# Fourteen scatter sends of the second part moved among the last attention slots, and the last batch's steps moved up to six slots later

## The chip, the core and the metric

The kernel runs on one core of one Trainium2 chip. TensorE multiplies matrices into PSUM, VectorE and ScalarE read PSUM and work elementwise, GpSimd works on SBUF and issues indirect DMAs, SyncE issues other DMAs. Each engine works through its own list of instructions in order; semaphores tie them together. The metric is the device time of one execution in microseconds (us).

## The reference

One transformer layer on x of 8 batches x 512 tokens x 128 channels: x = x + attention(layernorm(x)), then x = x + mixture(layernorm(x)).

```python
y = einsum('bnd,hde->bhne', x, Wkqv) + bkqv        # 16 heads; k and q of 128, v of 8
A = softmax(where(tril, q @ k.T / sqrt(128), -inf))
x = x + (A @ v).reshape(...) @ Wp + bp
# feed-forward on layernorm(x)
shared = (silu(x @ shared_gate.T) * (x @ shared_up.T)) @ shared_down.T
probs = sigmoid(x @ router_w.T + routing_bias)     # 8 experts
scores, indices = top_k(probs, 2); scores /= sum(scores)
combined = sum over the two picked experts of score * down(silu(gate(x)) * up(x))
x = x + shared + combined
```

## The kernel before

`prepare` loads and turns weights and is not touched. `body` holds everything else as one loop over slots `t`, from 0 to `SLOTS` = 215, written out once for each engine: an engine's list is what its code issues in slot 0, then in slot 1, and so on. Which step stands in which slot is fixed by tables of numbers; there is no scheduler.

**Attention**, slots 0 to 137. A unit is one head of one batch, 128 units. TensorE projects unit t in slot t (`project`), scores it for the row maxima one slot later, and scores it again ten slots later (`score`, three pieces, lines L1058 to L1060); VectorE takes the maxima (L1455), ScalarE the exponentials (L1327), GpSimd masks them in the same slot as the exponentials (L931 and L933). Every fourth slot, at `PV_AT + 4 g`, the value matmuls of four units follow (L1075, `weigh_values`); the last two groups stand in slots 135 and 139. They wait for the masks (`p_masked`). ScalarE copies their result (L1317) and stores it to `o_dram`. Slots 128 to 137 have no projection left.

**After attention, by batch.** When a batch's 16 heads are through, its steps run in slots `step_at(name, b)`: the gather of products and sums from DRAM, the inverse sums (`rinv`, L1514), their spread over partitions, the product (`mult`), the projection with Wp (`proj`, L1102) and its sum into x (L1394), the layer norm (`stats`, `aggr`, `newton0` to `newton2`, `norm` into `hn`), the split into two halves of 16 bits (`split`, into `rows`), and the router logits (`logits`). For the last batch, 7, the table is `LAST_STEPS`; its gather is issued by GpSimd (L946, L947), its spread is a matmul (L1108, step `spread`), its normalised rows are turned by TensorE (L1113, step `late`), copied in `late_copy`, and its exponentials (`exp`) are taken together with batch 6's on ScalarE, between two loads of the activation table.

**Routing, by part.** The tokens are cut into three parts of 12, 12 and 8 tiles of 128 (`SPLITS`). For each, VectorE picks two experts per token in seven steps (`sort`, L1552 to L1569), TensorE counts and ranks (`count`, L1132; `rank`, L1142 and on), VectorE works out each token's place (`place`, L1581 to L1600), and GpSimd scatters the rows to `xs_dram`, one indirect DMA (L969, a send) for each tile and pick: 24, 24 and 16 sends. `plan_sends` puts them in slots from `part_step_at("send", g)` on, two a slot before slot 138 and three in two slots after it. The scatter waits for `place_ready`; after slot 138 every second send also waits for TensorE's unit of the slot before (`gate_up`).

**Feed-forward**, slots 138 (`FFN_AT`) to 214. There are 69 units: 53 of routed rows, two tiles of 128 rows of one expert each, then 16 of the shared expert. A quad is four tiles; SyncE transposes its rows from `xs_dram` into a ring of four (L892). In slot 138 + u TensorE does the gate and up matmuls of unit u (`up`, L1164 to L1166, 12 matmuls) and the down matmuls of unit u - 4 (`down`, L1202 to L1204, 12 matmuls); ScalarE does Silu (L1358) and a rounding (L1363), VectorE a product (L1639) and a difference (L1642). ScalarE copies each finished quad out of its output bank (L1353) and stores it. Two output banks take turns by job, but the second also serves the small matmuls of the table `T_USES` and joins only after the last of these (`T_LAST`). `plan_fetches` then gives the 64 indirect DMAs that bring routed results back (L978, fetches) the places from `FETCH_AT` on that have no send, three in two slots; every second one of slots up to 207 waits for the unit of the slot before. VectorE adds each to x with its weight (L1610, two for a tile), those of the last eight tiles after the loop, and SyncE stores a batch when it is complete (L896).

## Time and profile before

| | |
|---|---|
| median of 3 runs | 705.58 us (703.97 to 706.2) |
| the profiled execution | 704.36 us, of which the span is 702.6 us |
| mean granted TensorE clock | 0.975 |
| busy share of the span | TensorE 91%, VectorE 77%, ScalarE 65%, GpSimd 44% |
| chain that ended last | TensorE 73%, VectorE 11%, issue 5%, ScalarE 4%, GpSimd 1% |

Times in the rows below are us from the start of the span. A row of a timeline has the start, the duration, the engine, the line, the operation, out<-in and a count, and in brackets how long the engine was idle before it and what ended that ("issue": nothing that the profile shows; "remote": no source known). PE is TensorE, DVE VectorE, ACT ScalarE, POOL GpSimd. Starts of matmuls are recorded, their ends are modelled. Slot 138's gate and up matmuls begin at 504.57.

### The profile page before, as it was taken

What the parts mean: (1) busy time and instruction counts of PE and PEld (TensorE: products, weight loads), DVE (VectorE), ACT (ScalarE), POOL (GpSimd) and SP (SyncE); (2) the same over time, 40 slices, a digit from 0 to 9 for tenths busy, and PEclk for the clock granted to TensorE, in tenths of its full rate; (3) what the DMA queues carried; (4) which work ended last, traced back from release to release, by engine and by line L of the source; (5) the groups of instructions that cost most, each with busy time, mean ns of one, the idle gap of its engine ahead of it and who ended that gap; (6) DMA issues with size and microseconds to landing.
All of it is one profiled execution on the core that took longest, in us unless ns stands there. A gap on an engine that the chain in (4) does not pass through costs nothing.

```text
span 702.6 us, 16427 instructions
## 1 busy us (share of the span) xinstructions
PE 638.1 (91%) x5432; PEld 402.7 (57%) x5432; DVE 538.8 (77%) x1903; ACT 456.4 (65%) x816; POOL 307.8 (44%) x511
## 2 busy tenths in 40 slices
PE   7489999999999999998999999999986788898983
PEld 7255555555555555554455555555565577786653
DVE  5799877798788878799878877878257745576886
ACT  3367776767767768776677866776745545565651
POOL 4393631323133223223478422422664276546673
PEclk9699999999999999999999999999999999999996
DMA  9200543621121112211241110211553376794424
GB/s 253 68 1 3 158 133 110 176 86 47 51 77 46 35 33 84 55 56 39 58 133 65 54 52 17 57 38 41 118 119 107 83 133 129 146 176 91 113 58 131
DMA packets 102768, 60.24 MB, mean 86 GB/s; under 512 B 44568, under 2 KB 94640, under 8 KB 102688
## 3 DMA queue, kind: packets, MB, share of 16 engines
q1 hardware_dynamic: 66144, 28.22, 16.7%
q10 hardware_dynamic: 32336, 22.29, 11.1%
q0 software_dynamic: 4208, 8.69, 4.8%
q8 instruction: 47, 0.77, 0.5%
q14 instruction: 33, 0.27, 0.1%
HBM read 19.62 MB, written 30.77 MB: 72 GB/s over the span
## 4 chain that ended last, share of the span: by engine, by line
PE 73%; DVE 11%; issue 5%; ACT 4%; another core or an unknown queue 1%; POOL 1%; ACTq 0%; DVEq 0%; POOLq 0%
PE bank L1058 9%; PE bank L1037 9%; PE bank L1075 9%; PE bank L1060 8%; PE bank L1059 8%; PE bank L998 4%; PE bank L1166 4%; PE bank L1000 4%; PE bank L999 4%; PE bank L1164 3%; PE bank L1165 3%; DVE junk L1455 2%; PE bank L1202 2%; PE bank L1204 2%; PE bank L1203 2%
## 5 line engine op out<-in xcount | busy, mean ns | idle before, releaser
L1327 ACT ACTIVATE p_sb<-bank,inv_scale 128x512 f32<-128x512 f32 (+1 forms) x384 | 222.1, 614 | 43.2 <-PE bank L1060 35.0
L1455 DVE CUSTOM_DVE_ANT_0 junk<-bank,causal 128x512 bf16<-128x512 f32 (+3 forms) x512 | 222.0, 483 | 29.0 <-PE bank L1037 27.5
L931 POOL TENSOR_SCALAR_AFFINE_SELECT p_sb<-p_sb 128x384 f32<-128x384 f32 x128 | 66.8, 522 | 280.3 <-ACT p_sb L1327 279.4
L1059 PE MATMUL bank<-ql,ah 128*128 128x512 f16 (+3 forms) x512 | 153.1, 299 | 0.0
L1060 PE MATMUL bank<-qh,al 128*128 128x512 f16 (+3 forms) x512 | 152.7, 299 | 0.0
L1058 PE MATMUL bank<-qh,ah 128*128 128x512 f16 (+3 forms) x512 | 146.9, 300 | 0.3 <-ACT p_sb L1327 0.3
L1037 PE MATMUL bank<-ah,qh 128*128 128x512 f16 (+3 forms) x512 | 130.1, 300 | 1.2 <-DVE low L1455 1.2
L1427 DVE TENSOR_TENSOR ql<-bank,qh 128x512 f16<-128x512 f32 x128 | 88.3, 690 | 42.8 <-ACT qh L1292 40.5
L1292 ACT ACTIVATE qh<-bank 128x512 f16<-128x512 f32 x128 | 76.4, 597 | 34.4 <-PE bank L1000 33.0
L1639 DVE SCALAR_TENSOR_TENSOR al<-bank,gu_scale,ah 128x512 f32<-128x512 f32 x69 | 51.6, 748 | 59.5 <-ACT ah L1358 43.1
L978 POOL DMA_INDIRECT p_sb<-ys_dram,place x64 | 67.9, 1061 | 39.6 <-PE bank L1166 17.4
L1358 ACT ACTIVATE ah<-bank,inv_gate 128x512 f32<-128x512 f32 x69 | 47.3, 686 | 58.3 <-PE bank L1166 32.9
L969 POOL DMA_INDIRECT xs_dram<-rows,place x64 | 65.6, 1024 | 40.5 <-issue 14.1
L1075 PE MATMUL bank<-p_sb,v_sb 128*9 128x512 f32 (+3 forms) x1024 | 74.9, 433 | 0.3 <-POOL p_sb L933 0.3
L1058 PEld LDWEIGHTS bank<-qh,ah 128*128 128x128 f16 x512 | 50.1, 98 | 38.5 <-issue 6.9
L1037 PEld LDWEIGHTS bank<-ah,qh 128*128 128x128 f16 x512 | 50.2, 98 | 35.4 <-issue 2.8
L1164 PE MATMUL bank<-mh,wh 128*128 128x256 f16 x212 | 59.4, 280 | 6.3 <-issue 4.7
L1060 PEld LDWEIGHTS bank<-qh,al 128*128 128x128 f16 x512 | 50.1, 98 | 24.9
L1166 PE MATMUL bank<-mh,wl 128*128 128x256 f16 x212 | 59.4, 280 | 3.4 <-issue 3.3
L1059 PEld LDWEIGHTS bank<-ql,ah 128*128 128x128 f16 x512 | 50.1, 98 | 20.5
L1202 PE MATMUL bank<-wh,qh 128*128 (+1 forms) x276 | 53.7, 227 | 8.5 <-issue 3.5
L1165 PE MATMUL bank<-ml,wh 128*128 128x256 f16 x212 | 59.3, 280 | 1.6 <-issue 1.4
(246 smaller groups left out, 1127.0 us busy)
## 6 DMA issues: line engine op xcount, KB each, us to landing
o_dram<-oT ACTq DMA_DIRECT2D x32, 256.0 KB, 2.3
ys_dram<-ql ACTq DMA_DIRECT2D x25, 256.0 KB
xs_dram<-causal ACTq DMA_DIRECT2D x6, 832.0 KB, 4.5
wst<-in_Wkqv SPq DMA_DIRECT2D x8, 264.0 KB, 5.0
x_sb<-in_x SPq DMA_DIRECT2D x8, 256.0 KB, 6.1
out<-x_sb SPq DMA_DIRECT2D x8, 256.0 KB
o_all<-o_dram SPq DMA_DIRECT2D x7, 256.0 KB
r_all<-r_dram SPq DMA_DIRECT2D x7, 256.0 KB
```

Source lines behind the costliest of these rows:

```text
L1037: last = nc.tensor.matmul(m.psum[M_BANK[k]][:, at:at + w], qh[:, u % RING, i * P:(i + 1) * P], m.ah[:, seg(b, N, w)], start=True, stop=True)
L1058: nc.tensor.matmul(bank, m.ah[:, keys], qh[:, s, c * P:N], start=True, stop=False)
L1059: nc.tensor.matmul(bank, m.ah[:, keys], ql[:, s, c * P:N], start=False, stop=False)
L1060: last = nc.tensor.matmul(bank, m.al[:, keys], qh[:, s, c * P:N], start=False, stop=True)
L1075: last = nc.tensor.matmul(m.psum[O_BANK][32 * j:32 * j + V1, c * P:N], m.v_sb[:, v // H * TB + c, v % H, :], p_sb[v % P_RING][:, P_AT[c]:P ...
L1164: nc.tensor.matmul(out, hi, x_h, start=True, stop=False)
L1165: nc.tensor.matmul(out, hi, x_l, start=False, stop=False)
L1166: return nc.tensor.matmul(out, lo, x_h, start=False, stop=True)
L1292: nc.scalar.activation(qh[:, t % RING, :], m.psum[Q_BANK][:, :], ACT.Copy).then_inc(qh_ready, 1)
L1327: nc.scalar.activation(p_sb[v % P_RING][:, S_AT[k]:S_AT[k] + S_WIDTH[k]], m.psum[S_BANK[k]][:, 0:S_WIDTH[k]], ACT.Exp, scale=m.inv_scale[: ...
L1427: nc.vector.tensor_tensor(ql[:, t % RING, :], m.psum[Q_BANK][:, :], qh[:, t % RING, :], ALU.subtract).then_inc(ql_ready, 1)
L1455: last = nc.vector.tensor_tensor_reduce(out=junk[:, S_AT[k] + at:S_AT[k] + at + w], in0=m.psum[M_BANK[k]][:, at:at + w], in1=m.causal[:, N ...
```

## The change

Only numbers that place steps change, and the engine of one step.

- Part 1 (the second) is sorted in slots 125 to 127 (before 127 to 131), counted in 128 (132), ranked and placed in 129 (136). Its 24 sends stand in slots 130 to 136 (two a slot, 14 in all) and 142 to 148 (ten); before, in 138 to 153.
- The last batch: spread in slot 145 (before 144), projection 146 (145), statistics 147 (145), aggregate 148 (145), Newton steps 149 and 150 (146), norm 150 (146), `late` 151 (147), `late_copy` 152 (148), logits 153 (149), exponentials 154 (150), split 154 (151).
- Part 2 (the last): sort in 155 and 156 (150 and 151), count 157 (152), rank 158 (153), place 159 (153), sends in 160 to 170 (154 to 164).
- Batch 6: projection in 132 (129), statistics 133 (131), norm 134 (133), and its norm is done by VectorE, not GpSimd.
- What follows by the planners: fetches in 171 to 213 (165 to 209), sums of the first 24 tiles in 181 to 210 (175 to 206), `T_LAST` 158 (153), so that nine jobs use the first output bank alone (before, seven).

```diff
-LAST_STEPS = {"gather": 1, "rinv": 2, "spread": 3, "mult": NEVER, "proj": 4, "stats": 4, "aggr": 4, "newton0": 5, "newton1": 5, "newton2": 5, "norm": 5, "late": 6, "late_copy": 7, "logits": 8, "exp": 9, "split": 10}
+LAST_STEPS = {"gather": 1, "rinv": 2, "spread": 4, "mult": NEVER, "proj": 5, "stats": 6, "aggr": 7, "newton0": 8, "newton1": 8, "newton2": 9, "norm": 9, "late": 10, "late_copy": 11, "logits": 12, "exp": 13, "split": 13}
 PART_STEPS = {"sort": 18, "weigh": 22, "count": 23, "rank": 27, "place": 27, "expert": 30, "send": 28}
...
+NEXT_PART_STEPS = {"sort": 16, "weigh": 24, "count": 19, "rank": 20, "place": 20, "expert": 24, "send": 21}
...
-QUIET = 2
+QUIET = 1
...
-            while at < 6 * FFN_AT and (FFN_AT - at // 6 <= QUIET or any(step_at("norm", b) == at // 6 for b in range(B))):
+            while at < 6 * step_at("gather", B - 1) and (FFN_AT - at // 6 <= QUIET or any(step_at("norm", b) == at // 6 for b in range(B - 2))):
                 at += 1
...
-                if (b := batch_at("norm", t)) is not None and b < B - 1:
+                if (b := batch_at("norm", t)) is not None and b < B - 2:
                     pool.wait_ge(rstd_ready, b + 1)
...
-                if (b := batch_at("norm", t)) == B - 1:
+                if (b := batch_at("norm", t)) is not None and b >= B - 2:
                     dve.wait_ge(rstd_ready, b + 1)
```

The lines of the changed kernel are eight further down in `body`, so L977 is its L969. GpSimd's list at the end of attention, before; the masks are those of slots 135 to 137, `xs_dram1` is part 1's buffer:

```order
L931 AFFINE_SELECT p_sb5<-p_sb5 128x3x128
L933 AFFINE_SELECT p_sb5<-p_sb5 128x128
L931 AFFINE_SELECT p_sb6<-p_sb6 128x3x128
L933 AFFINE_SELECT p_sb6<-p_sb6 128x128
L931 AFFINE_SELECT p_sb7<-p_sb7 128x3x128
L933 AFFINE_SELECT p_sb7<-p_sb7 128x128
L969 DMA xs_dram1<-rows,place 4864x256 x6
L946 DMA sums<-o_dram 128x1x64
L947 DMA o_all<-o_dram 128x1x512
L969 DMA xs_dram1<-rows,place 4864x256 x18
```

The same place after the change:

```order
L939 AFFINE_SELECT p_sb5<-p_sb5 128x3x128
L941 AFFINE_SELECT p_sb5<-p_sb5 128x128
L977 DMA xs_dram1<-rows,place 4864x256 x2
L939 AFFINE_SELECT p_sb6<-p_sb6 128x3x128
L941 AFFINE_SELECT p_sb6<-p_sb6 128x128
L977 DMA xs_dram1<-rows,place 4864x256 x2
L939 AFFINE_SELECT p_sb7<-p_sb7 128x3x128
L941 AFFINE_SELECT p_sb7<-p_sb7 128x128
L954 DMA sums<-o_dram 128x1x64
L955 DMA o_all<-o_dram 128x1x512
L977 DMA xs_dram1<-rows,place 4864x256 x10
```

Two sends now stand ahead of each mask, and ten are left behind the gather of the last batch.

VectorE's list from the last batch's sum into x to its normalised rows, before (slots 145 and 146; the Newton steps between are left out, the pair L1639 and L1642 is one unit's work):

```order
L1394 TENSOR_TENSOR x_sb<-bank,x_sb 128x512
L1523 BN_STATS bn<-x_sb 128x6 x4
L1527 BN_AGGR stats<-bn 128x2 x4
...
L111 TENSOR_TENSOR var<-var,rstd 128x4
L1639 SCALAR_TENSOR_TENSOR al<-bank,gu_scale,ah 128x512
L1642 TENSOR_TENSOR qh<-al,qh 128x512
L116 SCALAR_TENSOR_TENSOR tmp<-rstd,var 128x4
...
L1534 TENSOR_SCALAR rstd<-rstd 128x4
L1540 TENSOR_SCALAR hn<-x_sb,stats,rstd 128x128 x4
```

After the change, down to the first Newton step (slots 146 to 149):

```order
L1402 TENSOR_TENSOR x_sb<-bank,x_sb 128x512
L1647 SCALAR_TENSOR_TENSOR al<-bank,gu_scale,ah 128x512
L1650 TENSOR_TENSOR qh<-al,qh 128x512
L1531 BN_STATS bn<-x_sb 128x6 x4
L1647 SCALAR_TENSOR_TENSOR al<-bank,gu_scale,ah 128x512
L1650 TENSOR_TENSOR qh<-al,qh 128x512
L1535 BN_AGGR stats<-bn 128x2 x4
...
L111 TENSOR_TENSOR var<-var,rstd 128x4
L1647 SCALAR_TENSOR_TENSOR al<-bank,gu_scale,ah 128x512
L1650 TENSOR_TENSOR qh<-al,qh 128x512
L116 SCALAR_TENSOR_TENSOR tmp<-rstd,var 128x4
```

A unit's pair now stands between any two of the batch's steps, four where one stood.

GpSimd's last fetches, before, with what they wait for:

```order
L978 DMA p_sb5<-ys_dram2,place 128x128 [waits gate_up]
L978 DMA p_sb5<-ys_dram2,place 128x128
L978 DMA p_sb6<-ys_dram2,place 128x128 [waits gate_up]
L978 DMA p_sb6<-ys_dram2,place 128x128 x3
L806 UNCONDITIONAL_BRANCH
```

After the change:

```order
L986 DMA p_sb5<-ys_dram2,place 128x128 [waits gate_up]
L986 DMA p_sb5<-ys_dram2,place 128x128
L986 DMA p_sb5<-ys_dram2,place 128x128 [waits gate_up]
L986 DMA p_sb5<-ys_dram2,place 128x128 x5
L986 DMA p_sb6<-ys_dram2,place 128x128 x4
L814 UNCONDITIONAL_BRANCH
```

The same last wait for a unit, that of slot 207, now has nine fetches behind it, and three before.

## Rows read from the trace of the kernel before

**Rows 1.** Waits of TensorE, 440 to 600 us: total us, times, longest

```profile
PE bank L1113 <- DVE hn L1540: 4.2, 1, 4.2
PE bank L1132 <- DVE picked L1569: 2.9, 1, 2.9
...
PE bank L1202 <- ACT ql L1353: 2.1, 2, 1.4
...
PE bank L1108 <- DVE r_all L1519: 0.9, 1, 0.9
```

**Rows 2.** Timeline of TensorE: last value matmuls; slots 142, 152 (two rows), 156, 157

```profile
506.38 2.34 PE L1075 MATMUL bank<-p_sb,v_sb 128*9 128x512 f32 x32 [0.34 <-POOL p_sb L933]
...
515.26 0.28 PE L1164 MATMUL bank<-mh,wh 128*128 128x256 f16 x1 [1.17 <-DVE al L1639]
...
548.24 0.27 PE L1164 MATMUL bank<-mh,wh 128*128 128x256 f16 x1
...
550.62 0.23 PE L1202 MATMUL bank<-wh,qh 128*128 x1 [0.92 <-issue]
...
563.03 0.27 PE L1164 MATMUL bank<-mh,wh 128*128 128x256 f16 x1
...
565.01 0.27 PE L1164 MATMUL bank<-mh,wh 128*128 128x256 f16 x1
```

**Rows 3.** Stretches; busy PE, PEld, DVE, ACT, POOL; then clock, DMA share, GB/s

```profile
536.00:540.00 4.00, 3.72 (x29) 3.20 (x30) 1.74 (x4) 1.07 (x2) 0.00 (x0) 0.68 0.35 90
...
556.00:560.00 4.00, 3.73 (x31) 3.00 (x30) 2.44 (x6) 1.69 (x3) 0.00 (x0) 0.76 0.28 66
```

**Rows 4.** Timeline of GpSimd: masks of slots 131 and 137, a send of slot 147

```profile
492.15 0.54 POOL L931 TENSOR_SCALAR_AFFINE_SELECT p_sb<-p_sb 128x384 f32<-128x384 f32 x1 [3.22 <-ACT p_sb L1327]
...
505.56 0.52 POOL L931 TENSOR_SCALAR_AFFINE_SELECT p_sb<-p_sb 128x384 f32<-128x384 f32 x1 [0.91 <-ACT p_sb L1327]
...
534.91 0.96 POOL L969 DMA_INDIRECT xs_dram<-rows,place  x1 [0.30 <-issue]
```

**Rows 5.** Timeline of GpSimd: sends of part 0, the first of two slots

```profile
358.39 0.97 POOL L969 DMA_INDIRECT xs_dram<-rows,place  x1 [0.17 <-issue]
...
361.58 0.97 POOL L969 DMA_INDIRECT xs_dram<-rows,place  x1 [0.18 <-issue]
```

**Rows 6.** Timeline of VectorE: split, end of place, last batch, a pair, the sort

```profile
500.09 0.69 DVE L1419 SCALAR_TENSOR_TENSOR rows<-hn,rows 128x512 f16<-128x512 f32 x1 [7.13 <-ACT rows L1280]
...
503.71 0.18 DVE L1600 CAST place<-slot 128x24 int32<-128x24 f32 x1
...
529.22 0.68 DVE L1394 TENSOR_TENSOR x_sb<-bank,x_sb 128x512 f32<-128x512 f32 x1
...
535.02 1.11 DVE L1540 TENSOR_SCALAR hn<-x_sb,stats,rstd 128x128 f32<-128x128 f32 x4
...
547.29 0.75 DVE L1639 SCALAR_TENSOR_TENSOR al<-bank,gu_scale,ah 128x512 f32<-128x512 f32 x1 [2.80 <-ACT ah L1358]
...
548.55 0.19 DVE L1552 TENSOR_SCALAR ex<-ex 128x64 f32<-128x64 f32 x1
```

**Rows 7.** Timeline of ScalarE: last value copy; first table load and Silu of slot 150

```profile
512.42 0.60 ACT L1317 ACTIVATE oT<-bank 128x512 f32<-128x512 f32 x1 [4.92 <-remote]
...
543.13 1.28 ACT L1286 ACT_TABLE_LOAD   x1
...
546.57 0.69 ACT L1358 ACTIVATE ah<-bank,inv_gate 128x512 f32<-128x512 f32 x1
```

**Rows 8.** Timelines of GpSimd and VectorE at the end; landing of GpSimd's gather

```profile
685.42 0.94 POOL L978 DMA_INDIRECT p_sb<-ys_dram,place  x1 [0.99 <-remote]
...
692.67 0.95 POOL L978 DMA_INDIRECT p_sb<-ys_dram,place  x1 [0.30 <-issue]
...
694.60 4.29 DVE L1610 SCALAR_TENSOR_TENSOR x_sb<-p_sb,weight,x_sb 128x128 f32<-128x128 f32 x16
...
DMA to landing us min/median/max: 2.3/2.3/2.3
```

More of the change, by code:

```diff
@@ L454, with first_step @@
 NEVER = 10 ** 6
-LAST_STEPS = {"gather": 1, "rinv": 2, "spread": 3, "mult": NEVER, "proj": 4, "stats": 4, "aggr": 4, "newton0": 5, "newton1": 5, "newton2": 5, "norm": 5, "late": 6, "late_copy": 7, "logits": 8, "exp": 9, "split": 10}
+LAST_STEPS = {"gather": 1, "rinv": 2, "spread": 4, "mult": NEVER, "proj": 5, "stats": 6, "aggr": 7, "newton0": 8, "newton1": 8, "newton2": 9, "norm": 9, "late": 10, "late_copy": 11, "logits": 12, "exp": 13, "split": 13}
 PART_STEPS = {"sort": 18, "weigh": 22, "count": 23, "rank": 27, "place": 27, "expert": 30, "send": 28}
-LAST_PART_STEPS = {"sort": 9, "weigh": 10, "count": 11, "rank": 12, "place": 12, "expert": 13, "send": 13}
-SORT_LATE = ((0, 0, 0, 1, 2, 3, 4), (0, 0, 0, 0, 1, 1, 1))
+NEXT_PART_STEPS = {"sort": 16, "weigh": 24, "count": 19, "rank": 20, "place": 20, "expert": 24, "send": 21}
+LAST_PART_STEPS = {"sort": 14, "weigh": 19, "count": 16, "rank": 17, "place": 18, "expert": 19, "send": 19}
+SORT_LATE = (0, 0, 0, 1, 2, 3, 4), (0, 1, 2, 2, 2, 2, 2), (0, 0, 0, 0, 1, 1, 1)
+NEXT_STEPS = {**STEPS, "proj": 7, "stats": 8, "aggr": 8, "newton0": 8, "newton1": 9, "newton2": 9, "norm": 9}
+def first_step(b):
+    return PV_AT + H - GROUP + 2 + H * b
 def step_at(name, b):
     if (name, b) == ("logits", B - 2):
-        return step_at("rinv", b) - STEPS["rinv"] + LATE_LOGITS
-    return PV_AT + H - GROUP + 2 + H * b + (STEPS if b < B - 1 else LAST_STEPS)[name]
+        return first_step(b) + LATE_LOGITS
+    steps = STEPS if b < B - 2 else NEXT_STEPS if b == B - 2 else LAST_STEPS
+    return first_step(b) + steps[name]
 def part_step_at(name, g):
     b = SPLITS[g][1] // TB - 1
-    return step_at("rinv", b) - (STEPS if b < B - 1 else LAST_STEPS)["rinv"] + (PART_STEPS if b < B - 1 else LAST_PART_STEPS)[name]
+    return first_step(b) + (PART_STEPS, NEXT_PART_STEPS, LAST_PART_STEPS)[g][name]
 def sort_at(k, g):
-    return part_step_at("sort", g) + SORT_LATE[g == PARTS - 1][k]
+    return part_step_at("sort", g) + SORT_LATE[g][k]
 def batch_at(name, t):
```

## The prediction

> **What bounds the kernel now.** I read the page's shares first, then the waits of TensorE between 440 and 600 us, then the timelines of TensorE, GpSimd, VectorE and ScalarE from 484 to 570 us, and last GpSimd and VectorE from 685 us on. Up to 484 us the change moves nothing that matters. The weak part is the start of the feed-forward, slots 138 to 158 (a slot is one turn of the loop over `t`; unit u is in slot 138 + u). A unit costs TensorE 1.98 us when nothing is late (slots 156 and 157 start at 563.03 and 565.01), yet slot 142 starts at 515.26 and slot 152 at 548.24, 33.0 us for ten slots [rows 2]. TensorE, which works its list in order, waits there for single named things: 4.2 us for the normalised last batch (slot 147), 2.9 for the last part's picks (152), 0.9 for the last batch's inverses (144), and 2.1 for two copies on ScalarE, the longer 1.4 (slots 146 and 150) [rows 1]; a third such wait, 0.92 in slot 152, stands as issue [rows 2]. Behind the two long waits, in which TensorE was idle, the granted clock was 0.68 and 0.76 of full speed for 4 us each, a mix of the 2.4 and 1.2 GHz levels; that is 4 x 0.32 = 1.3 and 1.0 us lost [rows 3]. The end is bound elsewhere: GpSimd's fetches follow TensorE to the last one, and VectorE's last sums and the last store come behind them [rows 8].
>
> **Part one: fourteen sends go among slots 130 to 136.** In each slot up to 137 GpSimd masks one unit's exponentials, and the value matmuls of four units (L1075) need these masks. A send ahead of a mask delays it. Before, the last mask (slot 137) starts at 505.56 [rows 4] and the last value matmuls at 506.38 [rows 2], just behind it, and no send stands ahead. What two sends and a mask cost is seen where part 0's sends stand among attention slots: a pair starts at 358.39 and the next at 361.58, so 3.19 us a slot with GpSimd idle only for issue [rows 5]. From 492.15 (slot 131) to 505.56 (slot 137) a slot took 2.2 us [rows 4], so GpSimd becomes the bound. The places of part 1 must be there first. They now come from slot 129, not 136: its rank matmul can run at about 484 to 485, when VectorE's earlier work is through, and from there the chain takes 3.1 us (500.78, the end of the row at 500.09, to 503.89, [rows 6]): 487 to 489. Slot 130's two sends are then done before 492.15, when slot 131's exponentials let its mask start. Six slots of 3.19 follow: the last mask starts at 511.3 and is done at 512.1, and so the last value matmuls start 5.7 us late. Not all of it is felt. Before, ScalarE read their result only at 512.42 [rows 7], 3.7 us after they should have ended (506.38 + 2.34, [rows 2]), a lag that no row explains. Without it, the matmuls run from 512.1 to 514.4, the copy to 515.1, two steps of Silu and VectorE follow, and slot 142 starts at 518.6 and not 515.26: **+3.3 us**. If the lag stays it is +7; if GpSimd is quicker in the places where it waits anyway, +2. I take 3.3: TensorE will have idled ahead of these matmuls, and the lag came without such a pause. Batch 6's normalisation goes from GpSimd to VectorE (1.11 us, as the last batch's at 535.02), which is idle for 7.13 us in that place [rows 6]; the sends take more of GpSimd than that gives back, so it is worth nothing. The other ten sends, in slots 142 to 148, are used from slot 157 on, which did not wait for them before: nothing.
>
> One rule of the Trainium skill speaks against this step. In the rows, a send at 534.91 took 0.96 us [rows 4], the same as elsewhere, while VectorE normalised from 535.02 to 536.13 [rows 6]. The Trainium skill, SBUF — State Buffer, Who interferes with whom, says that a VectorE operation in a two-port mode locks GpSimd out of the ports through which it writes DMA descriptors, for the whole instruction. By it batch 6's normalisation in slot 134 would hold a send for up to 1.1 us and the sum would be 1.1 longer; the row shows no such hold, so the sum goes without.
>
> **Part two: the last batch's steps up to six slots later.** The wait for inverses (0.9) goes, as does probably the copy's 0.7 in slot 146. The 4.2 shrinks but stays. From the sum into x (slot 146) to the normalised batch (slot 150) VectorE has five pairs of unit work, 1.26 us each (547.29 to 548.55), and 5.6 of the batch's own (529.22 to 536.13 less the pair in it): 11.9 us [rows 6]. It starts that 2 to 3.2 us into slot 146. TensorE reaches the transposes of slot 151 after six units and the projection of about 0.9, 12.8 us. It waits 1.1 to 2.3, say 2.0, and of the 1.3 of slow clock I keep half, 0.7. Sum: 0.9 + 0.7 + 4.2 + 1.3 - 2.0 - 0.7 = **-4.4 us** (-3 if the wait stays, -7.1 if all goes).
>
> **Part three: the last part's sort, count and rank, slots 154 to 158.** Before: 1.4 + 0.9 + 2.9 and 1.0 of slow clock, 6.2 us. After, the exponentials stand in slot 154, the sort in 155 and 156, the count in 157. Two table loads and the exponentials hold ScalarE for 3.4 us (543.13 to 546.57, [rows 7]), as before, so VectorE starts on slot 154 about 5.2 us after TensorE does. Then it has a pair (1.26), the split (0.6), a pair, four sort steps (2.3), a pair and three steps (1.5): 8.2 us, and the picks are there at 13.4. TensorE, held 1.2 us in slot 156 because its banks wait for VectorE, gets to the count at 9.8 at the latest. It waits 3.6. The one slot more between exponentials and count is eaten by one more pair on VectorE. With the 1.2 and the clock's 1.0 that is 5.8. Two more jobs use the single output bank, since the other one serves the steps up to T_LAST, which goes from 153 to 158; each can wait for its copy as in slots 146 to 152, up to 1.4, and I take 0.4 each. So 6.6 against 6.2, **+0.4 us** (-2 to +2).
>
> Together TensorE is 0.7 us ahead at slot 159. From there to slot 206 both run the same units, and this reaches the tail.
>
> **Part four: the tail.** The last part's sends start in slot 160, not 154, and the fetches, which take the free places behind them, end in slot 213, not 209. From slot 208 on a fetch waits for no unit: three before, nine now, so six more stand behind the last units. Before, the sixth from the end starts at 685.42 on a wait for unit 67, and the last ends at 693.62: 8.2 us for six, 1.37 each and hardly less than 1.25 (0.95 and 0.30 of issue) [rows 8]. Now twelve follow that wait, 7.5 to 8.2 us more. Some is covered: VectorE's 16 last sums run from 694.60 without a pause, 0.27 each, so the last batch's eight began at about 696.8, 3.1 us after the last fetch, and did not wait [rows 8]. A small transfer by GpSimd took 2.3 us to land [rows 8], which leaves 0.8 of cover. Eight sums and the store follow as before: **+7.0 us** (+4.4 with all 3.1 as cover, +8.2 with none). TensorE's end and the other eight sums leave the critical path. SyncE gets no new wait: what is queued behind its wait for the last part's rows is only transposes of that part, whose rows leave by slot 170 for a unit of slot 176, 12 us of cover.
>
> For the landing, the Trainium skill, DMA: Bandwidth & Descriptors, Anatomy of one DMA, gives about 2.0 us plus bytes over 436 GB/s for a transfer issued by GpSimd. By this page my estimate is 2.15 us for a fetch of 64 KB, and the tail would be 6.9; no row shows a fetch land.
>
> **Sum.** 3.3 - 4.4 + 0.4 + 7.0 = +6.3 us, on the profiled execution's 704.36 (span 702.6 and 1.76 around it): **710.7**. The median of the runs shown is 705.58, 1.2 above the profiled one, so a median after may be that much higher too.
>
> **Rivals.** *Faster, all waits go.* If every step really comes to stand behind its inputs, the 7.1 of part two and the 6.2 of part three go, 13.3, against 3.3 and 7.0: -3.0 and 701.4. It decides from 12.4 us of waits removed. For it: one slot gives an input 1.98 us more. Against: VectorE's work in just these slots is longer than TensorE's. Chance 0.12. *No change.* The long wait vanishes and the table loads hide, 9 to 12 us of waits go and the fetches take the gain: 702.5 to 707.7, say 705.5. Chance 0.22. *Much slower.* The lag behind the last value matmuls stays, or the places come late: each us after 490 is one more for the last mask. Then 7 - 3 + 1 + 7 = +12, 716.4 at most, typically 714.5. Chance 0.18. *My forecast*, 707.7 to 713, has 0.48. That sends and fetches might not move is no rival: the order of instructions shows them moved.
>
> A measurement here can tell about 0.3% (2.1 us) from no change. Slower: 0.48 + 0.18 = 0.66; within: 0.22; faster: 0.12. The range leaves out most of the faster case and the end of the much slower one: 702.5 to 715.
>
> **What would show it.** The last value matmuls starting at 511 to 513 behind a mask show part one right, at 507 wrong. A wait of about 2 us for the normalised batch and of 3 to 4 us for the picks show parts two and three. Fetches that end about 16 us after the wait for unit 67, with VectorE idle before its last eight sums, show part four. If VectorE's last sums run on without a wait behind TensorE's last matmuls, the tail term is wrong and the forecast with it.

## The result and the profile after

The changed kernel takes 718.59 us (median of 4 runs, 716.81 to 720.37) beside 705.89 for the kernel before: a ratio of 1.0175, 95% interval 1.0142 to 1.0209. The forecast was 710.7, with 715.0 as its upper end. The profiled execution took 716.81 us with a span of 715.0, 12.4 more than the span before. The changed kernel's lines are eight further down. TensorE's waits, 440 to 600 us (compare [rows 1]: who was waited for, us in total, times, longest):

```profile
PE bank L1083 <- POOL p_sb L941: 6.3, 3, 3.4
PE bank L1210 <- ACT ql L1361: 3.5, 2, 3.2
PE bank L1140 <- DVE picked L1577: 2.9, 2, 2.4
...
PE bank L1121 <- DVE hn L1548: 1.4, 1, 1.4
```

The wait for the normalised batch fell from 4.2 to 1.4, the wait for inverses is gone, the picks' stayed. On top stands a new one: the value matmuls wait for GpSimd's masks. TensorE's timeline has the place (compare [rows 2]): the last two groups of value matmuls, slot 142, the last batch's transposes, slot 152, slot 154, the count, and slot 158:

```profile
502.33 4.03 PE L1083 MATMUL bank<-p_sb,v_sb 128*9 128x512 f32 x32 [2.59 <-POOL p_sb L941]
516.13 4.03 PE L1083 MATMUL bank<-p_sb,v_sb 128*9 128x512 f32 x32 [3.37 <-POOL p_sb L941]
524.34 0.27 PE L1172 MATMUL bank<-mh,wh 128*128 128x256 f16 x1
553.52 0.63 PE L1121 MATMUL bank<-ident,hn 128*128 128x128 f32 x4 [1.39 <-DVE hn L1548]
553.99 0.27 PE L1172 MATMUL bank<-mh,wh 128*128 128x256 f16 x1
560.96 0.39 PE L1172 MATMUL bank<-mh,wh 128*128 128x256 f16 x1 [2.28 <-issue]
573.28 0.22 PE L1140 MATMUL bank<-ones,picked 128*64 128x128 f16 x1 [2.38 <-DVE picked L1577]
573.59 0.28 PE L1172 MATMUL bank<-mh,wh 128*128 128x256 f16 x1
```

The last value matmuls start at 516.13 and not 506.38, and the 32 of them take 4.03 us instead of 2.34. The windows (busy PE, PEld, DVE, ACT, POOL, then clock, DMA share, GB/s; compare [rows 3]) say why: TensorE was idle for most of 512 to 516, and then the granted clock was 0.57 of full speed, close to the 1.2 GHz level.

```profile
512.00:516.00 4.00, 0.76 (x7) 0.43 (x5) 0.75 (x1) 2.18 (x3) 3.49 (x7) 1.00 0.14 47
516.00:520.00 4.00, 3.87 (x32) 1.21 (x32) 0.00 (x0) 0.00 (x0) 0.08 (x1) 0.57 0.01 2
```

GpSimd in the same place: the first send, the masks of slots 131, 134, 135 and 137, and two sends between them (compare [rows 4, 5]).

```profile
490.91 1.07 POOL L977 DMA_INDIRECT xs_dram<-rows,place  x1 [0.16 <-issue]
...
495.12 0.52 POOL L939 TENSOR_SCALAR_AFFINE_SELECT p_sb<-p_sb 128x384 f32<-128x384 f32 x1 [1.86 <-ACT p_sb L1335]
...
504.71 1.04 POOL L939 TENSOR_SCALAR_AFFINE_SELECT p_sb<-p_sb 128x384 f32<-128x384 f32 x1
...
506.17 0.98 POOL L977 DMA_INDIRECT xs_dram<-rows,place  x1 [0.17 <-issue]
507.45 0.96 POOL L977 DMA_INDIRECT xs_dram<-rows,place  x1 [0.30 <-issue]
508.93 0.52 POOL L939 TENSOR_SCALAR_AFFINE_SELECT p_sb<-p_sb 128x384 f32<-128x384 f32 x1 [0.52 <-issue]
...
515.31 0.53 POOL L939 TENSOR_SCALAR_AFFINE_SELECT p_sb<-p_sb 128x384 f32<-128x384 f32 x1
```

From slot 131 to 137 GpSimd takes 20.2 us, where it took 13.4 before. The tail, GpSimd and VectorE (compare [rows 8]): the last fetch that waits for a unit, the last fetch, and VectorE's last work.

```profile
690.10 0.95 POOL L986 DMA_INDIRECT p_sb<-ys_dram,place  x1 [1.69 <-remote]
...
703.87 0.94 POOL L986 DMA_INDIRECT p_sb<-ys_dram,place  x1 [0.30 <-issue]
```

```profile
704.33 0.75 DVE L1642 SCALAR_TENSOR_TENSOR x_sb<-bank,inv_down,x_sb 128x512 f32<-128x512 f32 x1 [7.57 <-remote]
705.00 1.39 DVE L1618 SCALAR_TENSOR_TENSOR x_sb<-p_sb,weight,x_sb 128x128 f32<-128x128 f32 x5
707.35 0.75 DVE L1642 SCALAR_TENSOR_TENSOR x_sb<-bank,inv_down,x_sb 128x512 f32<-128x512 f32 x1 [0.95 <-remote]
708.01 4.28 DVE L1618 SCALAR_TENSOR_TENSOR x_sb<-p_sb,weight,x_sb 128x128 f32<-128x128 f32 x16
```

Twelve fetches stand behind the wait at 690.10, as forecast, and they end at 704.8.

### The profile page after: what moved, and what is told of

It is laid out like the page before. It is cut to its first block and busy times, and to the rows that moved or that the text cites. A ratio compares the mean times of both kernels' runs of the same rounds, so it can differ in the third digit from the quotient of the medians.

```text
span 715.0 us, 16424 instructions
## 1 busy us (share of the span) xinstructions
PE 642.8 (90%) x5432; PEld 403.7 (56%) x5432; DVE 540.7 (76%) x1907; ACT 456.8 (64%) x816; POOL 304.3 (43%) x507
## 5 line engine op out<-in xcount | busy, mean ns | idle before, releaser
L977 POOL DMA_INDIRECT xs_dram<-rows,place x64 | 65.3, 1020 | 63.0 <-DVE place L1608 39.6
L1083 PE MATMUL bank<-p_sb,v_sb 128*9 128x512 f32 (+3 forms) x1024 | 78.3, 448 | 6.3 <-POOL p_sb L941 6.3
L1067 PEld LDWEIGHTS bank<-ql,ah 128*128 128x128 f16 x512 | 50.1, 98 | 20.5
L1083 PEld LDWEIGHTS bank<-p_sb,v_sb 128*9 128x9 f32 x1024 | 25.9, 93 | 62.5 <-issue 49.1
```

Source lines behind the costliest of these rows:

```text
L1067: nc.tensor.matmul(bank, m.ah[:, keys], ql[:, s, c * P:N], start=False, stop=False)
L1083: last = nc.tensor.matmul(m.psum[O_BANK][32 * j:32 * j + V1, c * P:N], m.v_sb[:, v // H * TB + c, v % H, :], p_sb[v % P_RING][:, P_AT[c]:P ...
```

## The experiments

The runs came in four groups, on three chips. The kernel before took 706.2 us beside e1 to e4, 678.7 beside e7 to e10, 708.3 beside e12 to e15 and 680.7 beside e18 to e20. Groups two and four ran on one and the same chip, on which attention takes as long as elsewhere but a unit of the feed-forward takes 1.98 us nearly throughout, where it takes 2.4 on the others. Ratios are therefore to the kernel before in the same group; they are those on record, and differ by up to 0.3% from the quotient of the two medians. Of the kernel before there is no trace on the chip with 1.98 us units; e19, which differs from it only in the order of fetches, stands in for it up to slot 168. e16, e11 and e17, the same kernels as e18, e19 and e20, gave no result. For the parts, milestones are read from TensorE's timelines as differences within one execution, so that they don't depend on how early it was: V is the start of the value matmuls of slot 131, ahead of all sends of part 1 (an expectation calls it slot 122), L that of the last ones (slot 139), 142, 152 and 168 are the starts of those slots, S the first send of the last part, F the end of the last fetch.

| kernel | ratio (interval) | L-V | 142-V | 142 to 152 | 152 to 168 | S | F | span |
|---|---|---|---|---|---|---|---|---|
| before, first profile | | 19.1 | 28.0 | 33.0 | 47.1 | 562.3 | 693.6 | 702.6 |
| before, e12 | | 19.1 | 27.8 | 34.7 | 47.9 | 565.6 | 696.3 | 705.2 |
| changed, first profile | 1.0175 | 26.7 | 34.9 | 29.7 | 47.1 | 582.3 | 704.8 | 715.0 |
| changed, e13 | 1.0144 (1.0103 to 1.0184) | 26.3 | 34.5 | 29.5 | 47.3 | 580.1 | 704.8 | 714.7 |
| e1 last only | 1.0058 (1.0034 to 1.0082) | 19.2 | 27.8 | 30.3 | 47.1 | 575.8 | 699.9 | 709.5 |
| e2 second only | 1.0145 (1.0096 to 1.0194) | 26.4 | 34.6 | 34.8 | 49.9 | 571.0 | 704.5 | 713.4 |
| e3 sends back | 1.0058 (1.0019 to 1.0097) | 20.1 | 28.7 | 30.8 | 46.0 | 574.5 | 699.5 | 709.7 |
| e4 dense fetch | 1.0271 (1.0215 to 1.0327) | 26.3 | 34.5 | 29.6 | 47.8 | 582.9 | 710.8 | 726.4 |
| e14 sends late | 1.0087 (1.005 to 1.0123) | 19.1 | 27.8 | 33.9 | 45.4 | 574.4 | 699.0 | 708.7 |
| e15 half late | 0.9999 (0.9975 to 1.0022) | 19.1 | 27.8 | 32.4 | 49.7 | 566.2 | 696.0 | 705.0 |
| *chip with 1.98 us units* | | | | | | | | |
| e19 before, 5/3 | 0.9998 (0.9974 to 1.0023) | 19.1 | 25.7 | 30.2 | 39.1 | 559.6 | 670.1 | 679.0 |
| e7 fetches late | 1.0145 (1.0108 to 1.0182) | 19.1 | 25.6 | 31.5 | 38.6 | 561.1 | 678.7 | 687.7 |
| e18 fetches late | 1.0114 (1.006 to 1.0169) | 19.1 | 25.7 | 30.3 | 39.1 | 558.1 | 676.4 | 685.4 |
| e8 changed, 5/3 | 1.0189 (1.0137 to 1.024) | 25.9 | 34.1 | 24.7 | 40.1 | 575.8 | 681.7 | 690.7 |
| e9 one send | 1.011 (1.008 to 1.0141) | 21.4 | 27.9 | 24.7 | 39.7 | 566.6 | 673.7 | 682.7 |
| e10 last only, 5/3 | 1.008 (1.005 to 1.011) | 19.1 | 25.7 | 24.7 | 39.8 | 566.4 | 672.3 | 681.2 |
| e20 half late, 5/3 | 0.9952 (0.993 to 0.9975) | 19.1 | 25.6 | 27.6 | 38.1 | 561.1 | 668.2 | 677.2 |

**The halves of the change.** e1 is the kernel before with the new `LAST_STEPS` and `LAST_PART_STEPS`, e2 the changed kernel with the old ones.

> Kernel before with only the last batch's and the last part's steps moved; the second part and batch 6 as before. If the masks behind the sends cost the 9 us up to slot 142, that slot starts near 515 here, the middle gains about 5 us and the fetches' shift costs 7.7 at the end: about +3 us against before. If moving the last batch's steps is what costs, it is +8 us or more.

> Changed kernel with the last batch's and the last part's steps put back, so only the second part's sort and sends and batch 6's norm differ from before. Masks behind sends: slot 142 starts near 524 and the fetches end as before, so +7 to +9 us. If the loss belongs to the last batch's steps: within 2 us of before.

e1 took 710.66 us beside 706.24, +4.4 (3 expected); e2 took 716.4, +10.2 (7 to 9 expected). The second part's half is much the dearer. In the table e2 is late by 6.6 us at slot 142 and e1 not at all. e2 is also 2 to 3 us longer than either profile of the kernel before between slots 152 and 168, as is e15; that stays open. V itself moves from one execution to the next: e1 has 489.31, e12 (the kernel before) 489.10 and the first profile after 489.44, while e2 and e13 have 487.60 and 487.65 and the first profile before 487.24. So 2.2 of the 9.1 us that slot 142 was late in the first pair of profiles belong to the execution, but for 0.3 us at most, a wait for a mask that stands ahead of V in all kernels with the early sort.

**Where in the second part.** e3 is the changed kernel with part 1's sends back in slots 138 to 153, its early sort kept; e9 the changed kernel with one send a slot among the attention slots.

```diff
-NEXT_PART_STEPS = {"sort": 16, "weigh": 24, "count": 19, "rank": 20, "place": 20, "expert": 24, "send": 21}
+NEXT_PART_STEPS = {"sort": 16, "weigh": 24, "count": 19, "rank": 20, "place": 20, "expert": 24, "send": 29}
-            while at < 6 * step_at("gather", B - 1) and ...
+            while at < 6 * FFN_AT and ...
```

```diff
-            at += 3 if at < 6 * FFN_AT else 4
+            at += (6 if g == 1 else 3) if at < 6 * FFN_AT else 4
```

> Changed kernel with the second part's 24 sends back in slots 138 to 153 and its sort still early. Masks behind sends: the last value matmuls start near 509 at full clock, 6 to 7 us sooner than in the changed kernel, and the time falls by about 6 us, to 712. If the early sort on VectorE is the cost, nothing changes: 718.

> The changed kernel with one edit: one send a slot in slots 130 to 136, not two (7 and not 14), the other 17 from slot 142 on. Theory (two sends and a mask are 3.4 us of GpSimd a slot, over the attention's 2.2 to 3, and that pace alone delays the last value matmuls): a send and a mask are 2.1 us and fit, the last value matmuls start 19.5 to 20.5 us after those of slot 122 (19.6 with the sends elsewhere, 26.7 with two a slot), slot 142 as with the sends in 138 to 153, and the time is 711 to 713. Rival (the delay comes from any indirect DMA among the attention slots, by its stay on GpSimd or on the DMA queue): half the delay stays, 715.

e3 took 711.77 us, e9 685.93 beside 678.66. What e3 keeps costs 0.7 to 0.9 us at slot 142, the fourteen sends the other 5.8 to 6.2. The rows put e3's own loss on batch 6's steps and not on the early sort: the mask of slot 131 still comes 4.9 us behind V, but batch 6 is normalised 1.0 us later than before, and ScalarE, which stands idle for it, gets to slot 135's exponentials that much later. e3, and the kernel before:

```profile
500.61 0.63 ACT L1288 ACTIVATE rows<-hn 128x512 f16<-128x512 f32 x1 [2.46 <-DVE hn L1548]
```

```profile
499.43 0.63 ACT L1280 ACTIVATE rows<-hn 128x512 f16<-128x512 f32 x1 [2.30 <-POOL hn L960]
```

TensorE's last value matmuls in e3, and in e9:

```profile
507.56 2.34 PE L1083 MATMUL bank<-p_sb,v_sb 128*9 128x512 f32 x32 [0.34 <-POOL p_sb L941]
```

```profile
508.72 2.34 PE L1083 MATMUL bank<-p_sb,v_sb 128*9 128x512 f32 x32 [0.78 <-POOL p_sb L941]
```

With one send a slot L-V is 21.4, 0.9 over the 19.5 to 20.5 expected, the wait for the mask is 0.8 and not 3.4, and the matmuls run at full clock, 2.34 us. So it is the sum of two sends and a mask, 3.2 us a slot against the attention's 2.2 in the mean, and not an indirect DMA as such, that holds TensorE. One send is not free either: in e9 most slots take 1.92 us from mask to mask, where ScalarE alone allows 1.68.

**The changed kernel again, and before again.**

> The kernel before, unchanged, for its trace on the chip of this group: the runs of e7 to e10 had the kernel before at 678.7 us and a unit at 1.98 us nearly throughout from slot 160 on, where the first traces have 2.4 us a slot and TensorE idle in the middle of units. Theory: if this chip is like that one, the fetches follow one another at about 1.3 us from slot 165 on with few waits for units, and the time is about 679; if it is like the first, 706 and fetches that wait for units every few slots.

> The changed kernel, unchanged, beside the kernel before on the same chip. Theory: where units run at 1.98 us, GpSimd works without a pause from the last part's first send to the last fetch, 80 indirect DMAs of about 1.3 us, 106 us, and the end comes 9 us behind it; the first send comes with the place of the last part, 575 to 576 (e8), so the span is 575.5 + 106 + 9 = 690 to 691 and the ratio 1.017 to 1.020. Where units run at 2.4 us: 1.0175 again. Rival (the ratio of the first measurement belongs to that chip's slow units): 1.01 or less on a chip with 1.98 us units.

e12 took 707.01 us in its one run; e13 716.44 beside 708.25. e13 has its V only 0.4 us behind that of the first profile before, so part one can be read off almost without a shift: L at 513.96, slot 142 at 522.12, 6.9 us behind 515.26. Its rows also show a piece that was not in the sum, here VectorE's normalisation of batch 6 and its split, then GpSimd in the same microseconds:

```profile
500.62 1.12 DVE L1548 TENSOR_SCALAR hn<-x_sb,stats,rstd 128x128 f32<-128x128 f32 x4
502.43 0.82 DVE L1427 SCALAR_TENSOR_TENSOR rows<-hn,rows 128x512 f16<-128x512 f32 x1 [0.70 <-ACT rows L1288]
```

```profile
500.33 0.97 POOL L977 DMA_INDIRECT xs_dram<-rows,place  x1 [0.18 <-issue]
501.61 0.96 POOL L977 DMA_INDIRECT xs_dram<-rows,place  x1 [0.30 <-issue]
502.58 1.04 POOL L939 TENSOR_SCALAR_AFFINE_SELECT p_sb<-p_sb 128x384 f32<-128x384 f32 x1
...
506.76 0.52 POOL L939 TENSOR_SCALAR_AFFINE_SELECT p_sb<-p_sb 128x384 f32<-128x384 f32 x1 [0.48 <-issue]
```

Five of the six slots take 3.17 to 3.20 us; the one that begins with the mask of 1.04 us takes 4.18. That mask lies beside the split and takes twice its usual time. The 0.48 us of idle time ahead of the next mask, which the profile doesn't name, ends with the exponentials that this mask reads (506.22 + 0.47 = 506.69). TensorE and ScalarE in the same place:

```profile
500.21 3.82 PE L1083 MATMUL bank<-p_sb,v_sb 128*9 128x512 f32 x32 [2.60 <-POOL p_sb L941]
```

```profile
504.07 0.60 ACT L1325 ACTIVATE oT<-bank 128x512 f32<-128x512 f32 x1 [1.67 <-PE bank L1083]
504.98 1.34 ACT L1335 ACTIVATE p_sb<-bank,inv_scale 128x512 f32<-128x512 f32 x2 [0.31 <-PE bank L1068]
...
506.22 0.47 ACT L1335 ACTIVATE p_sb<-bank,inv_scale 128x256 f32<-128x256 f32 x1
```

The value matmuls of slot 135 had waited 2.6 us for a mask and ran at the lower clock, 3.82 us and not 2.34; ScalarE's copy and slot 135's scores stand behind them. Slow mask and late exponentials are in e2 and in the first profile after as well.

**The tail.** e14 is the kernel before with its last places and sends six slots later and all else kept; e7 and e18 are the kernel before with only the fetches where the changed kernel has them.

```diff
-LAST_PART_STEPS = {"sort": 9, "weigh": 10, "count": 11, "rank": 12, "place": 12, "expert": 13, "send": 13}
+LAST_PART_STEPS = {"sort": 9, "weigh": 10, "count": 11, "rank": 12, "place": 18, "expert": 19, "send": 19}
```

```diff
-            x = max(x, -(-FETCH_AT[g] * 3 // 2))
+            x = max(x, -(-FETCH_AT[g] * 3 // 2), 257)
```

> The kernel before with the last part's places, and with them its sends, six slots later (places in 159, sends in 160 to 170, fetches in 171 to 213), and nothing else: the last batch's steps, sorts, counts and ranks stay. Theory (the end is GpSimd's chain of 16 sends and 64 fetches, so that each us by which the first send comes later is one at the end): the first send comes at 567 to 568 rather than 561 on a chip with 1.98 us units, slots 142 to 159 are as before, and the time is before + 7 to 9 us, ratio 1.010 to 1.013. Rival (only the fetches behind the last unit's wait matter, so that e7, with the sends early, already has all of it): the same as e7, 1.0145. Rival (SyncE's transposes of the last part come late for slot 176 and TensorE waits): more than 1.02.

> The kernel before with one edit: no fetch ahead of slot 171, so that all 64 fetches stand in exactly the slots that they have after the change (171 to 213, the last nine behind slot 208 with no unit to wait for); sends, sorts and steps stay. Theory (the tail is set by how many fetches stand behind the last one that waits for a unit): slots 142, 152 and 159 as before, the last gated fetch at about 685, twelve fetches of 1.25 us behind it, and the span 7 to 9 us longer: 713 to 715 beside 706. Rival 1 (the tail's cost in the changed kernel comes from the sends of the last part in slots 160 to 170, not from the fetches): no change, 705 to 707. Rival 2 (half of it is covered by VectorE's last sums): 709 to 711.

> The kernel before with no fetch ahead of slot 171, as e7. Theory for a chip with 2.4 us a slot (before at 705 to 708): the tail term is that of the fetches behind the last one that waits for a unit, twelve at 1.25 us and not six, 7 to 8 us less what VectorE's last sums cover, so before + 5 to 7, as e14 with the same fetch slots (+5.5). For a chip with 1.98 us a unit (before at 679): GpSimd never waits again once it is late, and it is before + 10, as e7. Rival (the cost is of the sends' place, and the fetches alone are free where units are slow): before + 0 to 2.

e14 took 713.76 us beside 708.25 (ratio 1.0087), e7 689.34 beside 678.66 (1.0145, 1.0108 to 1.0182) and e18 687.59 beside 680.69 (1.0114). In all three TensorE reaches slot 168, counted from V, within 1 us of the kernel before (e19 on the chip with 1.98 us units) or ahead of it, and the end is later all the same: the tail term is real, 5 to 11 us, and the fetches alone can carry it, since e7 and e18 leave the sends where they were. The one kernel gave 10.7 and 6.9 us on the one chip, with intervals that overlap. The fetches alone were tried only on that chip, and there they act in another way than was forecast: GpSimd waits 9.2 and 9.8 us for the unit ahead of its first fetch and hardly again, so that its whole chain starts late. Twelve fetches behind the last wait for a unit are seen on the other chips, with the sends moved too (the changed kernel, e1, e14). e14's +5.5 is below the 7 to 9 expected.

**A denser order of fetches.** e4 is the changed kernel with two fetches a slot, e8 with five in three slots, e10 is e1 and e19 the kernel before with five in three.

```diff
-            x = max(x, -(-FETCH_AT[g] * 3 // 2))
-            while sends_at(x * 2 // 3):
+            x = max(x, -(-FETCH_AT[g] * 5 // 3))
+            while sends_at(x * 3 // 5):
                 x += 1
-            slots[i] = x * 2 // 3
+            slots[i] = x * 3 // 5
```

> Changed kernel with two fetches a slot and not three in two slots, so that the last stands in slot 205 and none is left behind the last unit. If the fetches' place costs 7.7 us at the end, the time falls by 6 to 8 us, to about 711. If the end is bound by VectorE and the store, it stays at 718.

> The changed kernel with one edit: five fetches in three slots, not three in two, so that the last stands in slot 208 (before: 209, after: 213) and only two stand behind the last that waits for a unit. 5/3 x 1.25 us = 2.08 us of GpSimd a slot, beside 2.4 us that a slot takes from 171 to 206 in the changed kernel's trace; two a slot were 2.5 us, and that kernel was slower by 8 us. Theory (two a slot failed because GpSimd's 2.5 us a slot became the pace of all units, through VectorE's sums that wait for the fetched rows; below the pace of a slot a denser order gives the tail back): the last fetch ends 5 to 7 us sooner than in the changed kernel, 711 to 714 beside 718.6. Rival (any denser order holds VectorE up and with it TensorE): 718 to 722.

> The kernel before with the last batch's and the last part's steps of the changed one (that alone measured 710.7), and five fetches in three slots, the last in slot 208. Theory (the later steps give 4.2 us up to slot 159, and the tail takes 9 because of the fetches behind the last one that waits for a unit): with the tail as before, 702 to 705, faster than both kernels. Rival (the tail is set by when the last part's rows are stored and 16 fetches of 1.25 us behind that, however the rest stands): 707 to 711.

> The kernel before with five fetches in three slots, not three in two, the last in slot 207 and not 209, so that no fetch but one stands behind the last unit's wait. Theory (the end follows the last wait by the fetches behind it): three fetches fewer, 2 to 4 us faster where a slot takes 2.4 us; no change where units take 1.98 us, since GpSimd has no time left there. Rival (the sixteen fetches of the last part start only when its rows are stored, and denser fetches hold VectorE up, as with two a slot): 0 to 5 us slower.

e4's theory failed. It took 726.92 us, a ratio of 1.0271 (1.0215 to 1.0327), 8 more than the changed kernel. Its last part's first fetch waits 5.6 us for that part's rows, although it comes five slots sooner by the order:

```profile
689.13 0.94 POOL L986 DMA_INDIRECT p_sb<-ys_dram,place  x1 [5.62 <-DMA ys_dram<-ql]
```

TensorE was late. Its waits from 600 us to the end in e4 were nearly all unnamed, six groups that come to 19.4 us, the first of them:

```profile
PE bank L1172 <- issue: 4.8, 9, 1.1
```

In the changed kernel the same groups come to 12.0. e8 took 692.05 us and kept the changed kernel's loss (1.0189), e10 684.05 and kept e1's (1.008 beside 1.0058), and e19, 679.63 beside 680.69, gained nothing. Their gains had been forecast for 2.4 us a slot, and there five in three was never run; for units of 1.98 us e19's expectation said no change. On the chip of these three GpSimd's waits explain e8 and e10. In e9, from the last part's first send on, it waited for nothing but the issue of its own DMAs, once places were there:

```profile
POOL xs_dram L977 <- DVE place L1608: 26.7, 1, 26.7
POOL p_sb L986 <- issue: 19.5, 64, 0.3
POOL xs_dram L977 <- issue: 4.6, 15, 0.3
```

Its 80 indirect DMAs, 16 sends and 64 fetches, took 107.2 us (566.6 to 673.7), 1.34 each; 105.9 in e8 and e10, 107.1 in e20. The span ends 9.0 us behind the last fetch in each. So in these four the end is the first send + 115 to 116 us: 575.8 + 114.9 = 690.7 in e8, 566.4 + 114.8 = 681.2 in e10. A denser order can't help an engine that never pauses. In e19 it does pause, 4.9 us in three waits for units, the longest 4.3, and its chain takes 110.5 us; why the denser order gains nothing there is not shown, as the kernel before has no trace on that chip.

**Three slots later instead of six.** e15 is the kernel before with smaller steps; e20 is e15 with five fetches in three slots.

```diff
+LAST_STEPS = {"gather": 1, "rinv": 2, "spread": 4, "mult": NEVER, "proj": 5, "stats": 5, "aggr": 6, "newton0": 6, "newton1": 6, "newton2": 7, "norm": 7, "late": 8, "late_copy": 9, "logits": 10, "exp": 11, "split": 11}
+LAST_PART_STEPS = {"sort": 11, "weigh": 15, "count": 13, "rank": 14, "place": 14, "expert": 15, "send": 15}
```

> The kernel before with the last batch's steps up to three slots later, not six (projection in 146, logits in 151, sort in 152, count in 154, places in 155, sends in 156 to 166), so that the fetches of parts 1 and 2 stay in slots 183 to 209. Theory (the later steps take waits from TensorE, 4.2 us with six slots, and cost only what they put behind the fetches): TensorE is 2 to 4 us ahead at slot 159, the first send comes 0 to 2 us later than before, the last fetch at most 1 us later, and the time is between before - 3 and before + 1. Rival (all that delays the places delays the end, one for one): before + 2 to 3.

> The last batch's steps up to three slots later (e15, ratio 1.000) with five fetches in three slots, the last in slot 207. Theory: the 1 to 3 us that TensorE gains ahead of slot 159 and the three fetches fewer add up, before - 3 to - 5 where a slot takes 2.4 us. Rival: as for the kernel before with the same fetches, 0 to 5 us slower.

e15 took 707.17 us beside 708.25, no difference; it reaches slot 168 109.9 us behind V, between the 108.1 and 110.3 of the two profiles of the kernel before. e20 took 677.83 beside 680.69: 0.9952 (0.993 to 0.9975), faster than the kernel before by some 3 us, and the only one here that is. e19 shows that its fetch order alone is worth nothing there. TensorE is 3.5 us ahead at slot 168 (65.8 us behind slot 142 and not 69.3), and though the first send comes 1.5 later than in e19, GpSimd runs on without e19's waits: 107.1 us from first send to last fetch and not 110.5. On the other chips this version was not run.

## Why the prediction was wrong

The sum against three pairs: the first two profiles, e12 and e13, and, on the chip with 1.98 us units and with five fetches in three slots in both, e19 and e8. Part one is counted from V:

| term | predicted | first pair | e12, e13 | e19, e8 |
|---|---|---|---|---|
| V, not from the change | | +2.2 | -1.5 | 0.0 |
| part one, V to slot 142 | +3.3 | +6.9 | +6.7 | +8.5 |
| part two, 142 to 152 | -4.4 | -3.3 | -5.2 | -5.6 |
| part three, 152 to 168 | +0.4 | 0.0 | -0.6 | +1.0 |
| part four, from 168 | +7.0 | +6.7 | +10.0 | +7.7 |
| sum of the span | +6.3 | +12.4 | +9.4 | +11.6 |

**Part one is the step that failed**: +3.3 was forecast and 6.7 to 8.5 measured. Its mechanism was right: GpSimd became the bound of slots 131 to 137, the last value matmuls waited for a mask, and the places came in time. Its sizes were off, here in e13 against the first profile before. First, the six slots were counted from slot 131's mask at its old 492.15 [rows 4]; it came at 493.02. Of these 0.9 us 0.4 are the later V, and 0.5 come with ScalarE's copy ahead of that slot's exponentials, 2.8 us behind V and not 2.4, for a reason that the rows don't show (in e8 this piece is missing). Second, 3.19 a slot [rows 5] was taken for all six; one took 4.18, half by the slow mask beside the split and half by exponentials that stood behind slot 135's slowed value matmuls. Rows 5 come from a place with no such neighbours. Together the last value matmuls are 7.6 us late where 5.7 was said. Third, and largest: the sum counted that TensorE would idle ahead of these matmuls, and used the idling only to take the lag of 3.7 us before ScalarE's copy away. The lag did go, as ScalarE's timeline after shows, 0.07 us behind the end of the matmuls at 520.16:

```profile
520.23 0.60 ACT L1325 ACTIVATE oT<-bank 128x512 f32<-128x512 f32 x1 [6.02 <-PE bank L1083]
```

But the clock came down behind the idle time, and the matmuls took 3.9 to 4.0 us instead of 2.34, 1.6 us on the path. The chip with 1.98 us units shows this piece alone: from the start of the last value matmuls to slot 142 e8 takes 8.2 us, and the six kernels there whose matmuls ran at full clock take 6.5, just what the sum had (512.1 to 518.6). The price stood in [rows 3], where TensorE ran at 0.68 and 0.76 behind its other two long waits. 0.9 + 1.0 + 1.6 = 3.5, and 3.3 + 3.5 = 6.8 beside e13's 6.9. The upper bound of 7 for this term was thus nearly its value. The rest of the miss in the first pair is the 2.2 us by which V was late there and a smaller gain in part two.

Where the lag comes from is open, but the runs show where it is: 3.4 to 3.7 us in all six kernels of the 2.4 us chips whose matmuls had hardly waited (both profiles of the kernel before, e1, e3, e14, e15), under 0.1 in the four that had waited 3.4 us, and under 0.1 in every kernel on the chip with 1.98 us units. So the change had a lag to take away only on the slower chips. That is why part one costs 6.7 to 6.9 us there and 8.5 on the faster one.

Batch 6's normalisation was put at nothing because VectorE was idle in that place. e3 shows that it comes 1.0 us later there and costs as much; in the changed kernel the masks are later still, and it is hidden.

The case "much slower" had the right size for the wrong reason: the lag did not stay, and the places were not late beyond 490 (489.16, in an execution whose V is 2.2 us late).

**Part two** gave 3.3 us in the first pair, 5.2 in the second, 2.7 in e1 against the first profile before, and 5.5 where units take 1.98 us (e10 against e19); the kernel before itself took 33.0 and 34.7 us for these slots, so the 4.4 stands within the scatter. The batch's wait is 1.4 where 2.0 was said, but a copy's wait in `down` (L1210) grew to 3.2 us, where the prediction had 0.7 us of such waits go. **Part three** came out in its sum, and partly by luck. The picks' wait stayed, as VectorE's own work sits between exponentials and picks, but it was 2.4 us where 3.6 was said. A pause of 2.28 us ahead of slot 154 was not in the sum, and behind it the granted clock was 0.60 from 560 to 564. It stands in every kernel with the full new steps of the last batch (2.1 to 2.3) and, with 1.9, in e20, but not in e15. TensorE's sequencer, which feeds the engine, reads the table of experts just then, three loads from 558.3 to 560.3:

```profile
L1162 PEldq TENSOR_LOAD <-tile_expert x3: 295/304/702, 558.3 to 560.0; - x3
```

The kernel before has the same loads ahead of slot 154 (556.8 to 558.4), with 0.27 us of idle time behind them; why they are hardly felt there is left open. What hides both pieces in the first pair is that the kernel before lost time here too. A trap lay here: slot 159, at which the prediction drew its line, is no good mark. The kernel before has unnamed pauses between 566 and 573, behind its first sends of the last part; in the changed kernel these sends and pauses come behind slot 159. Slot 168 lies behind both. One window of the kernel before, in which TensorE was busy for 1.1 of 2 us:

```profile
568.00:570.00 2.00, 1.10 (x8) 0.63 (x8) 1.35 (x2) 0.53 (x2) 1.70 (x2) 1.00 0.55 138
```

**Part four** was right in size in the first pair, but not in mechanism, and there luck helped. Twelve fetches followed the last wait, at 1.25 us, as said; they took 14.7 us where six had taken 8.2, so +6.5. The prediction then let VectorE's last sums and the last store end the kernel, with 0.8 us of cover. In the kernel before they don't. GpSimd's closing instruction, a DRAIN, ends at 685.65 + 16.70 = 702.35, 8.7 us behind the last fetch's end, while SyncE, whose last wait is for the stores, is through at 701.4:

```profile
L806 POOLq DRAIN  x1: 16699/16699/16699, 685.6 to 685.6; - x1
...
L806 SPq DRAIN  x1: 13/13/13, 701.4 to 701.4; - x1
```

In all 17 traces this DRAIN ends 8.7 us behind the last fetch, and in 11 of them it is what ends the span. So there was no cover to count: what moves the last fetch moves the end. In the changed kernel it ends at 713.55, and the stores are later still, 714.8, because of something that wasn't forecast: all of VectorE's last 16 sums start only after the last fetch. Eight of them needed only earlier fetches, but stood behind sums (L1642) that waited 7.57 and then 0.95 us. The second of these starts at 707.35, just when TensorE's closing DRAIN ends (699.32 + 8.03), though TensorE's last matmul starts at 700.12:

```profile
L814 PEldq DRAIN  x1: 8030/8030/8030, 699.3 to 699.3; - x1
```

So VectorE waits for TensorE, and what holds TensorE there the profile doesn't name. e1, e3, e13 and e14 have such a wait too, 7.9 to 8.6 us, and in all five TensorE's DRAIN ends 1.9 to 2.6 us behind the last fetch. It adds 0.6 to 1.3 us to the span. On the chip with 1.98 us units it is missing, and eight sums run behind the last fetch, as predicted:

```profile
664.49 2.20 DVE L1618 SCALAR_TENSOR_TENSOR x_sb<-p_sb,weight,x_sb 128x128 f32<-128x128 f32 x8
675.30 2.19 DVE L1618 SCALAR_TENSOR_TENSOR x_sb<-p_sb,weight,x_sb 128x128 f32<-128x128 f32 x8 [8.61 <-DMA p_sb<-ys_dram,place]
```

The rows are e9's. Its span ends 5.2 us behind these sums, with GpSimd's DRAIN. These rows also give the landing: 2.5 us from the last fetch's start (672.80), 1.6 from its end, where 2.3 from its end had been taken.

In e13 the sends at 500.33 and 501.61 took 0.97 and 0.96 us, as anywhere, while VectorE normalised from 500.62 to 501.74. The Trainium skill, SBUF — State Buffer, Who interferes with whom, gives the ports to whichever of the two starts first, so the send at 500.33 would have held the normalisation, and not been held, if that ran in a two-port mode. The trace shows no hold: the normalisation took 1.12 us where it had taken 1.11 in the prediction's row, in which the send started first as well. No row tells the mode, and no row shown here has a send that starts well inside a normalisation. The sum was right to go without the term.

For the landing of a fetch the prediction's estimate from the Trainium skill, DMA: Bandwidth & Descriptors, Anatomy of one DMA, was 2.15 us; e9 has 2.5 from the start of its issue, so the trace roughly agrees.

## What to carry to other kernels

Where work on an engine is moved ahead of something that TensorE waits for, add two prices to the queueing: the slower clock on whatever TensorE does right behind the new idle time (1.6 us here behind a wait of 3.4), and the worst neighbour in the place itself, since a pace read elsewhere has other company. And before steps of one chain are moved later to save waits, add up the engine at the other end of the chain: here GpSimd had 80 indirect DMAs of 1.3 us to do after the last places, so that six slots more cost what they saved and more, while three slots cost nothing. And look up which instruction really ends the span before counting cover: here it was GpSimd's DRAIN, 8.7 us behind its last fetch, and not the last store.

## What was not expected of the hardware

The same kernel took 679 to 681 us on one chip and 706 to 708 on others, at nearly the same mean granted clock. V, at the end of attention, was at 487 to 490 us on all of them; the difference is in the feed-forward. From 600 to 640 us TensorE was busy for 39.4 of 40 us in e9 and for 35.8 in the changed kernel's first profile:

```profile
600.00:620.00 20.00, 19.38 (x233) 18.03 (x234) 15.46 (x29) 13.68 (x26) 15.43 (x16) 1.00 0.98 192
620.00:640.00 20.00, 20.00 (x200) 14.38 (x198) 18.15 (x38) 14.60 (x26) 15.38 (x16) 1.00 0.45 123
```

```profile
600.00:620.00 20.00, 18.01 (x214) 16.07 (x212) 11.72 (x18) 12.70 (x23) 11.59 (x13) 1.00 0.80 140
620.00:640.00 20.00, 17.76 (x195) 14.59 (x193) 11.82 (x20) 11.06 (x20) 14.10 (x13) 1.00 0.75 166
```

On the slower chips the missing time is idle time of TensorE between the matmuls of a unit, 0.2 to 1.5 us at a time, that no semaphore explains. It is thick from 5 to 9 us behind the first send of the last part and grew with two fetches a slot (e4); the faster chip moves as many bytes and has none of it. What it waits for was not settled.
